# A state-space kernel: the states' products as 64-row halves for two groups at a time, and taps kept as pairs of channels

## The reference, cut to what matters

```python
h = _layernorm(x) * (1 + ca) + sa
def step(h, x_t):                       # per channel d: 16 states
    h = einsum('dnm,bdm->bdn', A, h) + Bm[None] * x_t[..., None]
    y_t = einsum('dn,bdn->bd', Cm, h) + Dm * x_t
    return (h, y_t)
y = scan(step, ...)                     # 8192 steps, 512 channels
y = gelu(_layernorm(y) * ln_w + ln_b) @ W_out.T + b_out
x = x + ga * (h + y)
# then a small feed-forward part and a second residual
```

## Time and profile before

| | us |
|---|---|
| median of 3 runs | 956.12 |
| the runs | 953.27 to 958.15 |
| the profiled execution, whole | 956.1 |
| its span, first to last instruction | 954.4 |

### The profile page before, as it was taken

How to read it: one execution, slowest core, us unless ns; L and a number is a source line. 1 busy time by engine, 2 the same in 40 slices (tenths; PEclk the granted TensorE clock), 3 DMA queues, 4 the chain that set the end, 5 groups by cost and what they waited for, 6 DMA issues and landing times.

```text
span 954.4 us, 25074 instructions
## 1 busy us (share of the span) xinstructions
PE 872.5 (91%) x10267; PEld 555.3 (58%) x10267; DVE 594.6 (62%) x1263; ACT 421.4 (44%) x887; POOL 498.2 (52%) x643
## 2 busy tenths in 40 slices
PE   2999898999799998989959999999999999999984
PEld 2966877766599997856635444444444444444430
DVE  6678478633322238834664777777778777777654
ACT  2545631100011132100025777767677676777652
POOL 4544514644333341744548667766666677666610
PEclk9999689999855579999979999999999999999986
DMA  8944102188500001079850021222212222122111
GB/s 263 389 141 144 57 13 69 30 245 247 135 3 2 3 3 58 3 206 275 238 207 0 1 90 67 69 87 89 89 74 72 77 81 75 67 89 67 45 45 67
DMA packets 109810, 94.91 MB, mean 99 GB/s; under 512 B 14976, under 2 KB 81152, under 8 KB 109696
## 3 DMA queue, kind: packets, MB, share of 16 engines
q1 hardware_dynamic: 109696, 93.31, 31.0%
HBM read 75.99 MB, written 17.30 MB: 98 GB/s over the span
## 4 chain that ended last, share of the span: by engine, by line
PE 65%; issue 13%; DVE 10%; ACT 4%; POOL 3%; DMA 3%; SPq 1%; DVEq 0%; POOLq 0%; ACTq 0%
PE PS L1018 17%; PE PS L889 9%; PE PS L892 7%; PE PS L992 5%; PE PS L987 5%; PE PS L959 4%; PE PS L1051 3%; PE PS L1029 3%; PE PS L867 3%; PE PS L1040 2%; ACT arenaA L524 2%; DMA arenaC<-kernel_taps 2%; PE PS L1008 2%; DVE arenaA L745 2%; DVE arenaC L636 1%
## 5 line engine op out<-in xcount | busy, mean ns | idle before, releaser
L1018 PE MATMUL PS<-arenaC,arenaA 128*128 128x512 f32 x512 | 240.1, 602 | 1.2 <-ACT arenaA L515 1.2
L353 POOL TENSOR_TENSOR arenaC<-arenaA,par 128x512 f32<-128x512 f32 x104 | 107.6, 1039 | 144.6 <-ACT arenaA L477 69.7
L889 PE MATMUL PS<-arenaA,arenaC 64*64 64x17 f32 (+6 forms) x1792 | 162.4, 263 | 22.1 <-DVE arenaC L636 22.1
L821 DVE SCALAR_TENSOR_TENSOR ROWS<-arenaA,ffc,ROWS 128x256 f32<-128x256 f32 x240 | 141.7, 590 | 24.6 <-DVE ROWS L821 1.4
L892 PE MATMUL PS<-arenaA,arenaC 64*64 64x1 f32 (+6 forms) x1792 | 154.1, 241 | 0.0
L889 PEld LDWEIGHTS PS<-arenaA,arenaC 64*64 64x64 f32 x1792 | 138.0, 194 | 27.5 <-issue 23.2
L542 ACT ACTIVATE arenaA<-PS,ffc 128x256 f32<-128x256 f32 x256 | 129.6, 575 | 29.7 <-PE PS L1040 18.4
L1018 PEld LDWEIGHTS PS<-arenaC,arenaA 128*128 128x128 f32 x512 | 90.9, 192 | 83.5 <-issue 81.9
L892 PEld LDWEIGHTS PS<-arenaA,arenaC 64*64 64x64 f32 x1792 | 139.1, 194 | 0.0
L636 DVE STREAM_TRANSPOSE arenaC<-arenaC 128x512 f32<-128x512 f32 x104 | 73.5, 707 | 94.5 <-POOL arenaC L353 89.1
L403 POOL TENSOR_TENSOR arenaC<-arenaA,mask 128x504 f32<-128x504 f32 x64 | 66.9, 1046 | 75.9 <-PE PS L987 73.5
(11 more groups left out here) (144 smaller groups left out, 1239.5 us busy)
## 6 DMA issues: line engine op xcount, KB each, us to landing
arenaC<-kernel_taps SPq DMA_DIRECT2D x64, 512.0 KB, 4.3
arenaC<-in_L_attn_x SPq DMA_DIRECT2D x20, 512.0 KB, 4.7
out<-arenaC SPq DMA_DIRECT2D x20, 512.0 KB, 2.7
arenaC<-in_L_attn_x SPq DMA_DIRECT2D x32, 256.0 KB, 4.0
XY<-in_L_attn_x SPq DMA_DIRECT2D x32, 256.0 KB, 4.3
XY<-in_L_wmod SPq DMA_DIRECT2D x6, 1024.0 KB, 8.8
arenaA<-in_L_attn_x SPq DMA_DIRECT2D x12, 512.0 KB, 4.4
out<-arenaA SPq DMA_DIRECT2D x12, 512.0 KB, 2.8
```

Source lines behind the costliest of these rows:

```text
L353: gp.tensor_tensor(BDs[:, step % BDR, :, :].rearrange("p g (a m) -> p g a m", m=NS), src, msk, ALU.mult).then_inc(S["bdp_r"], 1)
L821: ins = dve.scalar_tensor_tensor(out=g, in0=rr[:, h % RELU_RING, :], scalar=W2c[:, h:h + 1], in1=g, op0=ALU.mult, op1=ALU.add)
L889: pe.matmul(pv_ps(r)[e:e + BW, j, 0:w + NS], BDTs[e:e + BW, b, j, :], PV[e:e + BW, g, PW - w:PW + NS], start=True, stop=True)
L1018: pe.matmul(PS[:, 2 + t, :], zT[:, u % 2, q, t * P:(t + 1) * P], WoT[:, q, :], start=(q == 0), stop=False)
```

## The change

In the save of the taps and its tensor, channels stand in pairs: `kscr` is (256 pairs, 256 positions, 2 channels). Five DMAs take the place of one in each half: four write the taps of the even or the odd channels of one block of 128, each value of 4 bytes on its own at a step of 8 bytes, and one writes the zeros. The load of a group reads, for each partition and each of four pairs, one run of 256 values (1024 bytes), and line 992 takes its weights from it with a step of two. `BDH` is 4 x 64 columns a group with four slots. The states' products are made for two groups at a time, as four products of 64 rows by 256 columns in two rounds, with a wait on `o_mm` between the rounds.

```diff
-    kscr = nc.dram_tensor("kernel_taps", [D, 2 * L], f32, kind="Internal").ap()
+    kscr = nc.dram_tensor("kernel_taps", [D // 2, 2 * L, 2], f32, kind="Internal").ap()
...
-        BDH = UR.rearrange("p (r h c) -> p r h c", r=2, h=GC)
-        Tring = C0[:, 5120:8192].rearrange("p (r h i) -> p r h i", r=3, h=GC)
+        BDH = UR.rearrange("p (r h c) -> p r h c", r=4, h=4)
+        Tring = C0[:, 5120:8192].rearrange("p (r h i a) -> p r h i a", r=3, h=GC // 2, a=2)
...
-                    sp.wait_ge(S["o_mm"], half * HG)
+                    sp.wait_ge(S["o_mm"], 2 * half * HG)
                     sp.wait_ge(S["bdh_r"], half * HG)
                     load_A(half)
 
                 sp.wait_ge(S["kt_r"], 2 * (half + 1))
-                sp.dma_start(kscr[half * HD:(half + 1) * HD, :].rearrange("(b p) w -> p b w", p=P), ktz).then_inc(S["k_saved"], 16)
-                sp.wait_ge(S["k_saved"], 16 * (half + 1))
+                with nc.allow_non_contiguous_dma(reason="taps of two channels side by side"):
+                    for b in range(2):
+                        first = (half * 2 + b) * M
+                        for a in range(2):
+                            sp.dma_start(kscr[first:first + M, 0:L, a], ktz[a:P:2, b, 0:L]).then_inc(S["k_saved"], 16)
+                tail = kscr[half * P:(half + 1) * P, L:2 * L, :].rearrange("i w a -> i (w a)").rearrange("i (b x) -> i b x", b=2)
+                sp.dma_start(tail, ktz[:, :, L:2 * L]).then_inc(S["k_saved"], 16)
+                sp.wait_ge(S["k_saved"], 80 * (half + 1))
...
-                    row = (half * HG + g) * GC
-                    src = bass.AP(kscr.tensor, row * 2 * L, [[1, P], [2 * L, GC], [1, L]])
-                    sp.dma_start(Tring[:, n % 3, :, :], src).then_inc(t_ld[n % 3], 16)
+                    src = bass.AP(kscr.tensor, n * GC * 2 * L, [[2, P], [4 * L, GC // 2], [1, 2 * L]])
+                    sp.dma_start(Tring[:, n % 3, :, :, :].rearrange("p h i a -> p h (i a)"), src).then_inc(t_ld[n % 3], 16)
...
-                    if g >= 2:
-                        gp.wait_ge(S["o_mm"], n - 1)
-                    gp.tensor_tensor(BDH[:, g % 2, :, 1:NC], PV[:, g, H0:H0 + NC - 1].unsqueeze(1).to_broadcast([P, GC, NC - 1]),
-                                     mask8[:, :].unsqueeze(2).to_broadcast([P, GC, NC - 1]), ALU.mult).then_inc(S["bdh_r"], 1)
+                    if g >= 4:
+                        gp.wait_ge(S["o_mm"], 4 * ((n - 4) // 2 + 1))
+                    gp.tensor_tensor(BDH[:, g % 4, :, 1:NC], PV[:, g, H0:H0 + NC - 1].unsqueeze(1).to_broadcast([P, 4, NC - 1]),
+                                     par4[:, :].unsqueeze(2).to_broadcast([P, 4, NC - 1]), ALU.mult).then_inc(S["bdh_r"], 1)
...
-                    if g >= 4:
-                        pe.wait_ge(S["y_ev"], n - 3)
-                    pe.wait_ge(S["bdh_r"], n + 1)
                     if g == 0:
                         pe.wait_ge(S["bz_r"], half + 1)
-                    pe.matmul(PS[:, g % 4, :], WP[:, g, 0:L], BDH[:, g % 2, :, :], start=True, stop=False,
-                              skip_group_check=True).then_inc(S["o_mm"], 1)
+                    if g % 2 == 0:
+                        if g >= 4:
+                            pe.wait_ge(S["y_ev"], n - 2)
+                        pe.wait_ge(S["bdh_r"], n + 2)
+                        for i in range(2):
+                            if i:
+                                pe.wait_ge(S["o_mm"], 2 * n + 2)
+                            for e in range(2):
+                                gi, ci = g + e, slice(256 * (i ^ e), 256 * (i ^ e) + 256)
+                                ri = slice(BW * (i ^ e), BW * (i ^ e) + BW)
+                                pe.matmul(PS[:, gi % 4, ci], WP[ri, gi, 0:L], BDH[ri, gi % 4, :, :], start=(i == 0), stop=False,
+                                          skip_group_check=True).then_inc(S["o_mm"], 1)
                     pe.wait_ge(t_ld[n % 3], 16 * (n // 3 + 1))
                     for h in range(GC):
                         for a in range(0, P, 64):
-                            mm = pe.matmul(PS[a:a + 64, g % 4, h * NC:(h + 1) * NC], Tring[:, n % 3, h, a:a + 64], channel(n * GC + h),
-                                           start=False, stop=(h == GC - 1), skip_group_check=True)
+                            mm = pe.matmul(PS[a:a + 64, g % 4, h * NC:(h + 1) * NC], Tring[:, n % 3, h // 2, a:a + 64, h % 2],
+                                           channel(n * GC + h), start=False, stop=(h == GC - 1), skip_group_check=True)
                     mm.then_inc(S["t_mm"], 1)
```

More of the change, by code:

```diff
@@ L378, in _ @@
                         else:
-                            gp.wait_ge(S["o_mm"], half * HG)
+                            gp.wait_ge(S["o_mm"], 2 * half * HG)
                         chain(gp.memset(CM, 0.0))
@@ L459, in _ @@
                 if half:
-                    act.wait_ge(S["o_mm"], half * HG)
+                    act.wait_ge(S["o_mm"], 2 * half * HG)
                     act.wait_ge(S["bdh_r"], half * HG)
```

## The result

The changed kernel takes 1320.7 us (median of three runs, 1317.8 to 1330.1) against 956.9 before; the ratio is 1.383, 95% interval 1.374 to 1.393. A fourth run, whose granted clock was 0.66 where the three have 0.79 to 0.80, took 1435.4 us and is left out of the median and the ratio. The profiled execution has a span of 1315.9 us against 954.4: 361.5 us more, where 18 less were forecast.

The account below looks back on a forecast made before the run. PE was taken to bound the output stage, with the loads of taps not far behind. Savings of 10.9 us in the first half and 6.9 in the second, 17.8 from 956.1, gave 938.3 us; range 926 to 962.

Parts of the forecast that it names:

- The save of the taps: Five DMAs saving taps, 2048 packets per DMA engine: 8.5 ns each, 17.4 us, hidden before the first loads.
- the slow rival: Save at 46 ns a 4-byte write delays the first T by 45 and 47 us: 1030 us; chance 0.11.
- The room: Time for the save before first taps are needed: 49.6 and 47.4 us, free up to about 22 ns a packet.
- The landing of the taps: Output stage's tap loads land after about 3.77 us where 3.12 are allowed: 0.33 us stall, a pair 3.74.
- rival 2: Ring of three takes the gain: landing 5.0, stall 0.93, a pair 4.34 us, time 956; chance 0.06.
- PE: Output stage: S for two groups 1.37 us, a pair of groups 3.41 against 4.30 without any other limit.
- rival 1: Row halves of the states' products don't run side by side: a pair 4.27 us, time about 955.5; chance 0.11.
- Stepped weights: T's weights read with a step of two in the output stage: zero cost, as the weights are hidden.
- rival 3: T's weights load at half speed: a pair 4.98 us, time 975; chance 0.06.
- POOL: POOL's block of 252 columns a partition takes about half of 1.03 us and stays hidden.
- The second half and the last stage: Group 26 put out at 465.7, 6.9 us earlier; DVE's 13.8 us behind it unchanged, last stage as before.
- The ends of the case: Forecast's case runs from 928 us with no stall to 948 us with a stall of 0.65 a pair.

Follow-up runs that it names:

- The run into SBUF: Changed kernel with pairs put together by four DMAs of 4-byte pieces from SBUF to SBUF, then one save of 2048-byte rows: 958.3 us, ratio 1.002.
- the run at a step of 64 bytes: Kernel before plus 16384 unread 4-byte pieces to DRAM in each half, step 8 bytes in the first, 64 in the second: 1093 us.
- the run with the plain save: Changed kernel with the taps saved by one DMA in contiguous runs of 1024 bytes, so y is wrong: 955.1 us, ratio 0.998.
- the half loads: New states' products on the old taps' layout, each load bringing four of eight channels, so y is wrong: 938.0 us, ratio 0.980 to before.
- one more buffer place: New states' products on the old taps' layout, with a fourth place for taps in the first half only: 944.5 us, ratio 0.987 to before.
- The kernels with 16384 more pieces: Kernel before plus 16384 unread pieces to DRAM beside each save, of 4, 16 or 64 bytes at various steps: 1093, 1047 and 962 us.

## Why the prediction was wrong, point by point

**The save of the taps: the step that failed.** The prediction set its cost between 8.5 ns (4 bytes read into SBUF) and 46 ns a piece (1024 bytes written), took the lower, and gave the slow rival 0.11. Measured are 125 and 99 ns: outside both bounds. The reason given, that "size and not direction made the price", came from reads of 4 and 512 bytes and a contiguous write of 1024; it was carried to writes of 4 bytes at a step of 8, and there it is false. The run into SBUF (16 ns) and the run at a step of 64 bytes (32 ns) show what was missing: the target in DRAM and the distance between pieces. And a long write is no upper bound for a short one. The room was rightly worked out, 22 ns a piece: at 16 ns no T waited for it.

The slow rival named the right place; its price was 92 us and should have been some 370. Its path, the wait on `k_saved`, is only a part. PE began the states' products at 390.05 instead of 184.73 and would have been about as late without that wait, as its idle time ahead of T was only 5.3 us, and 10.8 in the second half. That the small writes keep PE itself from going on is a term that the prediction put at nothing, and it gave no row for that.

By the Trainium skill, "DMA: Bandwidth & Descriptors", Specifications, a transfer under 512 bytes is a read-modify-write. The runs agree in direction for writes to DRAM, 155 ns for 4 bytes against 46 for 1024; in the write into SBUF, 16 ns, nothing of it is seen.

**The landing of the taps: a term mis-sized.** Predicted were 3.77 us to landing and 0.33 us of stall a pair; the run with the plain save has 4.7 us, and with a pair of 4.30 on the mean (15 pairs, 185.73 to 250.28 us) where 3.56 are PE's own, the stall is 0.74. Two things were wrong. The packet of 1024 bytes was priced by its usual 46 ns in a write, and takes 54 on the mean when the taps are read. And the 4.1 us of before were measured with one load asked for every 2.15 us; now they are asked for in twos, about 1 us apart, and then 2.5 us nothing. So the pair is as long as it was. That is rival 2, which had a chance of 0.06, its 956 against 955.1 measured.

**PE: right.** Row halves side by side, so rival 1 falls. S for two groups 1.43 for 1.37; the pair without waits 3.45 for 3.41. When the loads were made light, 938.0 came out, where the prediction had 938.3 with full loads; the agreement is partly chance, as the half loads still waited a little.

**Stepped weights:** 0.05 us a group, for zero; rival 3 (0.8) falls. By the rule of the Trainium skill that the prediction cites for this the cost was nothing; the measurement, small and seen in two runs, decides.

**POOL:** 0.61 us for a block of 252 columns and not about 0.52, hidden as predicted.

**The second half and the last stage:** DVE's tail behind group 26 was 13.8 us and is 13.0 after (836.75 to 849.76), and the last stage 466.1 for 468.0. Both nearly as said.

**The ends of the case:** the 1.1 us in the sum of the fast end have no row behind them, and a stall of 0.65 gives 947 and not 948 by the prediction's own terms. Neither decides anything.

## What to carry to other kernels

A row bounds only what it has in common with the new operation: for a DMA that is its size, its direction, its target and how close the pieces lie. If the page shows no small writes to DRAM, put the rearrangement on the way into SBUF, or measure first. Before a stage's engine is made faster, work out the lead that its prefetch has left, with the landing times' spread and not with their median: here one more buffer place was worth 10 us, and the faster products alone 3. And ask of a transfer not only who waits for it, but what else runs on the DMA engines meanwhile: in this kernel the instructions of PE did.

## What the runs showed of the hardware that was not expected

Small writes to DRAM hold up PE, though it does not wait for them. In the changed kernel PE's scan products (line 964) sat idle for 195.7 us with nothing but "issue" to wait for:

```profile
L964 PE MATMUL PS<-arenaA,arenaC 64*64 64x80 f32 x1536 | 104.5, 300 | 207.6 <-issue 195.7 <-DVE arenaA L1100 8.5 <-DVE arenaA L756 2.8
```

The same products had 11.1 us of idle time before. The DMA queue that brings instructions had 7 packets of 16 KB from 138 to 376 us, 1.6% of 16 engines' 238 us, 8.7 us each (the rows in the first section). From 200 to 240 us of the kernel before it had 5, at 0.9% of 40 us, 1.2 us each:

```profile
q8 instruction: 5, 0.08, 0.9%
```

So PE reached the output stage only at 390 us. A save that nobody waits for would have been no way out.

The kernels with 16384 more pieces show it with nothing else changed. In the one with a step of 8 bytes the taps' loads go out at 291.56, and PE begins the states' products only at 310.41 (184.73 before), so it is not the taps that it is late for. Its waits from 133 to 290 us, and that start:

```profile
PE PS L942 <- issue: 64.6, 9, 58.5
PE PS L966 <- issue: 38.1, 6, 29.3
...
310.41 1.13 PE L994 MATMUL PS<-arenaC,arenaA 128*128 128x512 f32 x2 [0.82 <-DVE arenaA L1095]
```

The idle time marked "issue" and the time of an instruction packet go with the price of the pieces (a few packets each, so the last column is rough):

| small writes | stretch, us | PE idle with "issue", us | us an instruction packet |
|---|---|---|---|
| none, kernel before | 133 to 185 | 0 | 1.1 |
| 4 bytes at 8, to DRAM | 133 to 290 | 103 | 6.9 |
| 4 bytes at 16, to DRAM | 393 to 483 | 51 | 5.8 |
| 4 bytes at 32, to DRAM | 134 to 198 | 27 | 4.1 |
| 4 bytes at 64, to DRAM | 487 to 521 | 9 | 2.4 |
| 64 bytes at 128, to DRAM | 136 to 152 | 0 | 1.3 |
| 4 bytes at 8, into SBUF (32768) | 134.5 to 167 | 4 | 2.9 |

That small writes to DRAM hold PE up is shown by these runs. That they do it through the instruction queue, which shares the DMA engines with them, is the likely reason and not shown by itself. The clock is low meanwhile. This stretch of the changed kernel (us, busy by engine, PEclk, DMA share, GB/s) has PE busy for 78 of 258 us and a granted clock of 0.61:

```profile
136.00:394.00 258.00, 77.75 (x1068) 62.79 (x1066) 45.20 (x113) 12.10 (x34) 24.27 (x26) 0.61 1.31 2
```

Of the two levels, 2.4 and 1.2 GHz, it was the lower for most of it.
